# A four-layer graph network on one core: the edge network of the middle layers kept on 128 partitions

## The chip, the cores and the metric

The kernel runs on one core of one Trainium2 chip, in one launch. The metric is the device time of that launch in microseconds (us). Engines are called by the profile's names: PE is TensorE (PEld its weight loads), DVE VectorE, ACT ScalarE, POOL GpSimd, and SPq, ACTq and POOLq are the queues on which DMAs are issued.

## What is computed

Four graph layers update `x` (3125 nodes x 160 values: 64 scalars and 32 vectors of three) over 100,000 edges sorted by `dst`. Each adds its result to `x`. The two middle layers, L1 and L2, do per edge, with `k` = 8 and 16 features of the edge (L1 shown, L2 differs in scale factors and in a mean in place of a sum):

```python
h = silu(edge_scalars @ fcW1 * (1.0 / np.sqrt(RAD)))      # edges x 8 -> edges x 64
w = h @ fcW2 * (1.0 / np.sqrt(HID))                       # -> edges x 192
wA, wB, wC, wD = (w[:, :64], w[:, 64:128], w[:, 128:160], w[:, 160:192])
xs, xv = f_s[edge_src], f_v[edge_src]                     # the node's row, gathered
outA = wA * xs * y0
outD = wD * jnp.einsum('eud,ed->eu', xv, y1) * INV3
outB = wB[:, :, None] * xs[:, :, None] * y1[:, None, :]
outC = wC[:, :, None] * xv * y0[:, :, None]
agg = segment_sum(concatenate([outA, outD, outB, outC]), edge_dst)   # 384 values an edge
```

`h` and `w` are the inner values and the outputs of the "edge network". All is fp32.

## The kernel before

Edges are cut into 784 tiles of 128, with 48 more tiles that repeat edges at window borders. Four tiles make a group: 208 groups in L1 and L2, 196 in L3. The order of all work is written by hand: each engine has its own program, and `unrolled(count, [(lag, stage), ...])` lays out for step i every stage for group i - lag. Semaphores tie the engines together.

For a group g of L1 or L2 the engines do this:

- SP loads the edge features to `W.attr` (k x 512), two buffers.
- POOL gathers the node rows, `gathers_by_src` with the `indirect_dma_start` of L624: four gathers a group, each 128 rows of 640 bytes, to one of `DEPTH` = 4 buffers `W.got` in `fore`. Before a group's first gather it waits until the messages of four groups earlier are done. In L3 it does eight gathers a group, from `src_table` and `dst_table`, by the same line.
- PE has three stages, in this order in a step: `sums_by_window` for group i (L1233, four products 128 x 384 over 128 partitions, which add messages by destination; L1 has 384 columns, L2 385), `weights_by_hidden` for group i+2 (L1214, four products 128 x 192 over 64 partitions, giving `w`), `hidden_by_scalars` for group i+3 (L1200, one product 64 x 512 over 8 or 16 partitions, giving `h` before silu). In the trace each fp32 product shows as two weight loads and two matmuls ("passes" below).
- ACT does `hidden_out` (L848, silu from PSUM bank 0 to `W.hid`) and `rows_by_y0` (L864, four scalings of gathered rows).
- DVE (`edges_by_window`; its products go through a helper, L1446) makes the messages from `w` and the rows, and adds window sums to the accumulator. Every 32 windows (16 groups) it loads the next window numbers to registers.

PSUM: bank 0 holds the hidden product, banks 1 and 2 or 3 and 4 the weights (`wmm(b)`, two tiles to a bank), banks 5 to 7 the window sums.

L0 runs before them with a like loop, whose sums are scattered by POOL (L662); L3 after them, with two tensor products and an attention. At the start of the kernel ACT issues all weight loads (`wload`, L723) before the first square root of the layer norm (`root`, L715), for which DVE waits. `BY_Y0` splits `fc2_1` and `fc2_2` into four column pieces each.

## Time and profile before

| | |
|---|---|
| median of 3 timed runs | 7715.1 us (7669.87 to 7729.05) |
| profiled execution, span | 7980.6 us |
| mean granted TensorE clock | 0.904 |
| busy: PE, DVE, POOL, ACT | 88%, 82%, 67%, 46% |

The only time of the profiled execution is its span, from its first to its last instruction. It is 265.5 us (3.4%) above the median of the timed runs, which ran without the profiler. By stage of the program the profile has: set-up to about 130 us, L0 to about 1930, L1's edges from 2067 to 3185, L2's from 3313 to 4430, L3's from 4600 to 7350, L3's second pass and the end to 7980.6.

### The profile page before, as it was taken

How to read it: one execution, taken by the hardware profiler on the slowest of the kernel's cores; microseconds unless marked ns; L12 is line 12 of the kernel's file. 1: busy time of each engine (PE TensorE's matmuls, PEld its weight loads, DVE VectorE, ACT ScalarE, POOL GpSimd, SP SyncE). 2: the span in 40 equal slices, each digit the busy share in tenths (PEclk: the TensorE clock that was granted, in tenths of full speed). 3: DMA queues.
4: the chain of work that ended last, by engine and by line, in shares of the span. 5: the costliest groups of instructions: out<-in, count | busy, mean ns of one | idle time of the engine just before them, and what ended most of it. 6: DMA issues, size and time to landing. Idle time of an engine off the chain costs nothing. (4 is left out here: it accounts for less than half of the span.)

```text
span 7980.6 us, 110610 instructions
## 1 busy us (share of the span) xinstructions
PE 7037.4 (88%) x32406; PEld 4813.5 (60%) x32406; DVE 6580.0 (82%) x18417; ACT 3693.0 (46%) x9602; POOL 5364.8 (67%) x4078
## 2 busy tenths in 40 slices
PE   6999999997999999899999788888888888888488
PEld 3444444444555555555555477777787777777366
DVE  7999999996788888688888677777787777777785
ACT  2444444443333333433333355555555555555385
POOL 1777777773577777377777188888888888887000
PEclk7999999996899999799999778888888888888698
DMA  7999999998222222122222133322222222222263
GB/s 211 167 168 170 167 169 165 166 162 189 52 65 66 66 65 61 37 68 69 69 69 69 32 68 76 73 68 71 73 76 69 74 70 72 72 72 71 68 192 107
DMA packets 459687, 776.87 MB, mean 97 GB/s; under 512 B 96721, under 2 KB 310966, under 8 KB 458838
## 3 DMA queue, kind: packets, MB, share of 16 engines
q0 software_dynamic: 274944, 469.50, 32.1%
q1 hardware_dynamic: 180038, 299.69, 12.3%
q8 instruction: 269, 4.41, 0.2%
q14 instruction: 324, 2.65, 0.1%
q10 hardware_dynamic: 4112, 0.62, 0.1%
HBM read 464.60 MB, written 304.85 MB: 96 GB/s over the span
## 5 line engine op out<-in xcount | busy, mean ns | idle before, releaser
L1446 DVE TENSOR_TENSOR work<-work 128x256 f32<-128x256 f32 (+5 forms) x5726 | 2483.9, 472 | 70.3 <-DMA work<-src_sum 27.6
L624 POOL DMA_INDIRECT fore<-node_table,src_i x1664 | 1709.7, 1027 | 655.9 <-issue 504.4
L662 POOL DMA_INDIRECT src_sum<-work,put_i x832 | 1325.2, 1593 | 557.1 <-ACT work L836 384.6
L624 POOL DMA_INDIRECT fore<-src_table,src_i x784 | 1218.3, 1554 | 406.8 <-issue 238.6
L624 POOL DMA_INDIRECT fore<-dst_table,dst_i x784 | 1090.0, 1390 | 238.9 <-issue 238.9
L1233 PE MATMUL bank<-work 128*128 128x384 f32 (+1 forms) x3328 | 1198.8, 503 | 10.4 <-DVE work L1446 10.4
L1330 PE MATMUL bank<-ident,work 128*128 128x128 f32 x4704 | 733.5, 297 | 444.4 <-DVE work L1446 444.4
L1233 PEld LDWEIGHTS bank<-work 128*128 128x128 f32 x3328 | 603.2, 191 | 688.2 <-issue 313.6
L1446 DVE TENSOR_TENSOR work<-work,bank 128x384 f32 (+6 forms) x2080 | 908.0, 437 | 78.4 <-issue 70.7
L1330 PEld LDWEIGHTS bank<-ident,work 128*128 128x128 f32 x4704 | 572.3, 151 | 566.7 <-DVE work L1446 506.0
L848 ACT ACTIVATE work<-bank 64x512 f32<-64x512 f32 x416 | 245.8, 591 | 1436.6 <-PE bank L1200 1436.6
L1185 PE MATMUL bank<-work 128*128 128x480 f32 x1664 | 780.4, 604 | 3.0 <-DVE work L1446 2.8
L1446 DVE TENSOR_TENSOR work<-fore 128x640 f32<-128x640 f32 (+1 forms) x198 | 166.9, 843 | 621.7 <-DMA fore<-dst_table,dst_i 599.9
L1214 PEld LDWEIGHTS bank<-w_fc,work 64*128 64x128 f32 x3328 | 532.7, 188 | 237.8 <-issue 225.7
L1214 PE MATMUL bank<-w_fc,work 64*128 64x192 f32 x3328 | 656.1, 338 | 5.4 <-ACT work L848 5.4
L836 ACT ACTIVATE work<-bank 128x480 f32<-128x480 f32 x832 | 474.4, 570 | 303.0 <-PE bank L1185 236.6
L1446 DVE TENSOR_TENSOR work<-bank,aux 128x128 f32<-128x128 f32 (+1 forms) x1248 | 606.8, 487 | 0.0
L1446 DVE TENSOR_TENSOR work<-bank,work 128x256 f32<-128x256 f32 x832 | 405.7, 488 | 218.6 <-ACT work L864 218.6
L1185 PEld LDWEIGHTS bank<-work 128*128 128x128 f32 x1664 | 272.2, 192 | 519.3 <-issue 266.3
L864 ACT ACTIVATE work<-fore,y 128x160 f32<-128x160 f32 x1664 | 570.6, 415 | 0.0
L979 ACT ACTIVATE work<-bank 128x768 f32<-128x768 f32 x392 | 324.5, 828 | 488.0 <-PE bank L1330 487.9
L1200 PE MATMUL bank<-work,w_fc 8*64 8x512 f32 (+1 forms) x832 | 449.2, 619 | 14.8 <-DMA work<-in_edge_attr 14.8
(246 smaller groups left out, 13200.5 us busy)
## 6 DMA issues: line engine op xcount, KB each, us to landing
edge_h<-work SPq DMA_DIRECT2D x196, 320.0 KB, 2.3
work<-edge_h SPq DMA_DIRECT2D x196, 320.0 KB, 3.4
work<-keys SPq DMA_DIRECT2D x196, 256.0 KB, 5.8
fore<-node_table,src_i POOLq DMA_INDIRECT x1664, 2.7
work<-in_edge_attr SPq DMA_DIRECT2D x196, 128.0 KB, 5.9
src_sum<-work SPq DMA_DIRECT2D x4, 6240.0 KB, 37.5
work<-src_sum SPq DMA_DIRECT2D x100, 240.0 KB, 4.3
src_sum<-work,put_i POOLq DMA_INDIRECT x832, 5.9
```

Source lines behind the costliest of these rows:

```text
L624: return pool.indirect_dma_start(dst, None, table, bass.IndirectOffsetOnAxis(ap=idx, axis=0), bounds_check=bound, oob_is_err=True)
L662: pool.indirect_dma_start(src_sum[t], bass.IndirectOffsetOnAxis(ap=put_i[:, e:e + 1], axis=0), E.run[:, g % 2, t * 480:(t + 1) * 480], Non ...
L836: act.activation(E.run[:, b, t * f:(t + 1) * f], bank[:, 6 + n % 2, 0:f], ACT.Copy).then_inc(s.run_out, 1)
L848: act.activation(W.hid[0:64, b, :], bank[0:64, 0, :], ACT.Silu, scale=(8 ** -0.5, 0.25)[l - 1]).then_inc(s.hidden_out, 1)
L864: last = act.activation(W.by_y0[:, b, t, :], W.got[:, g % DEPTH, t, :], ACT.Copy, scale=y[:, e:e + 1, 0])
L979: act.activation(T.t1[:, h % 2], bank[:, 1:3, 0:384], ACT.Copy).then_inc(s.m1_in_sbuf, 1)
L1185: nc.tensor.matmul(bank[:, 6 + n % 2, 0:f], E.sel[:, b, t, :], E.msg[:, b, t * f:(t + 1) * f], start=True, stop=True).then_inc(s.run_mm, 1)
L1200: nc.tensor.matmul(bank[0:64, 0, :], wt[f"fc1_{l}"][:], W.attr[0:k, b, :], start=True, stop=True).then_inc(s.hidden_mm, 1)
L1214: last = nc.tensor.matmul(wmm(b)[:, t, 0:192], W.hid[0:64, b, t * P:(t + 1) * P], wt[f"fc2_{l}"][:], start=True, stop=True)
L1233: last = nc.tensor.matmul(o, W.sel[:, b, t, :], W.msg[:, b, t * f:(t + 1) * f], start=t == 2 * i, stop=t == 2 * i + 1)
L1330: last = nc.tensor.transpose(bank[:, to + t, i * P:(i + 1) * P], f[:, b, at + t, c0:c0 + P], ident[:])
L1446: return V_.tensor_tensor(o, p, q, op)
```

## The change

The inner values of the middle layers lay on 64 partitions by 512 edges. They now lie on 128 partitions by 256: edges 0 to 255 of a group on partitions 0 to 63, edges 256 to 511 on 64 to 127.

- `hidden_by_scalars`: two products of 64 x 256 in place of one of 64 x 512. The second writes PSUM partitions 64 to 127, so it uses the other half of the array's columns.
- `hidden_out`: one activation of 128 x 256 in place of 64 x 512.
- `weights_by_hidden`: the same four products, now in the order of tiles 0, 2, 1, 3. Tiles 0 and 1 read partitions 0 to 63, tiles 2 and 3 partitions 64 to 127, so by turns the upper and the lower half of the array's rows. Tiles 0 and 1 write one PSUM bank, 2 and 3 the other.
- `fc2_1` and `fc2_2` need their 64 rows on both halves: 128 partitions, and each piece loaded twice, eight more DMAs on ACT's queue at the start.

```diff
@@ weights
-        weight("fc2_1", 64, 192)
+        weight("fc2_1", P, 192)
-        weight("fc2_2", 64, 192)
+        weight("fc2_2", P, 192)
@@ window_views
-            v.hid = g(2, 512)
+            v.hid = g(2, 256)
@@ scalar engine, weight loads
-                for to, at, n in BY_Y0:
-                    n = min(n, wt[name].shape[1] - to)
-                    wload(wt[name][:, to:to + n], a[key][:, at:at + n])
+                k = a[key].shape[0]
+                for row in range(0, wt[name].shape[0], k):
+                    for to, at, n in BY_Y0:
+                        n = min(n, wt[name].shape[1] - to)
+                        wload(wt[name][row:row + k, to:to + n], a[key][:, at:at + n])
@@ hidden_out
-                    act.activation(W.hid[0:64, b, :], bank[0:64, 0, :], ACT.Silu,
+                    act.activation(W.hid[:, b, :], bank[:, 0, 0:256], ACT.Silu,
@@ hidden_by_scalars
-                    nc.tensor.matmul(bank[0:64, 0, :], wt[f"fc1_{l}"][:], W.attr[0:k, b, :], start=True, stop=True).then_inc(s.hidden_mm, 1)
+                    for half in range(2):
+                        last = nc.tensor.matmul(bank[64 * half:64 * half + 64, 0, 0:256], wt[f"fc1_{l}"][:],
+                                                W.attr[0:k, b, 256 * half:256 * half + 256], start=True, stop=True)
+                    last.then_inc(s.hidden_mm, 1)
@@ weights_by_hidden
-                    for t in range(GROUP):
-                        last = nc.tensor.matmul(wmm(b)[:, t, 0:192], W.hid[0:64, b, t * P:(t + 1) * P], wt[f"fc2_{l}"][:],
+                    for t in (0, 2, 1, 3):
+                        rows, at_hid = slice(64 * (t // 2), 64 * (t // 2) + 64), t % 2 * P
+                        last = nc.tensor.matmul(wmm(b)[:, t, 0:192], W.hid[rows, b, at_hid:at_hid + P], wt[f"fc2_{l}"][rows],
                                                 start=True, stop=True)
```

On PE, at the third and fourth group of L1, the program before has this order (L1200 hidden, L1214 weights, L1233 sums):

```order
L1200 MATMUL bank<-work,w_fc1_1 64x512
L1233 MATMUL bank<-work 128x384 x4
L1214 MATMUL bank<-w_fc2_1,work 128x192 x4
L1200 MATMUL bank<-work,w_fc1_1 64x512
L1233 MATMUL bank<-work 128x384 x4
```

The changed program at the same place (L1203 hidden, L1220 weights, L1239 sums):

```order
L1203 MATMUL bank<-work,w_fc1_1 64x256 x2
L1239 MATMUL bank<-work 128x384 x4
L1220 MATMUL bank<-w_fc2_1,work 128x192 x4
L1203 MATMUL bank<-work,w_fc1_1 64x256 x2
L1239 MATMUL bank<-work 128x384 x4
```

No stage moved past another; the hidden product became two of half the columns, and the four products of a weights stage differ in the partitions they read, which such rows do not show.

On ACT, among the weight loads at the start, this piece of the difference is the only one in which rows are added:

```order
 L723 DMA w_fc2_1<-in_L1_gnn_fcW2 64x64
 L723 DMA w_fc2_1<-in_L1_gnn_fcW2 64x32
+L723 DMA w_fc2_1<-in_L1_gnn_fcW2 64x64
+L723 DMA w_fc2_1<-in_L1_gnn_fcW2 64x32
+L723 DMA w_fc2_1<-in_L1_gnn_fcW2 64x64
+L723 DMA w_fc2_1<-in_L1_gnn_fcW2 64x32
+L723 DMA w_fc2_2<-in_L2_gnn_Wfc2 64x64
+L723 DMA w_fc2_2<-in_L2_gnn_Wfc2 64x32
+L723 DMA w_fc2_2<-in_L2_gnn_Wfc2 64x64
+L723 DMA w_fc2_2<-in_L2_gnn_Wfc2 64x32
```

Eight DMA issues more stand ahead of everything that ACT does later, the first square root (L715) among it.

## Rows read from the trace of the kernel before

**Rows 1.** Windows: L0, middles of L1 and L2, L3; us busy per engine.

```profile
core 0: us, PE busy (x) PEld busy (x) DVE busy (x) ACT busy (x) POOL busy (x), PEclk, DMA share, GB/s
130.00:1920.00 1790.00, 1672.20 (x5479) 838.97 (x5479) 1708.66 (x6888) 828.83 (x1473) 1325.16 (x832) 0.97 0.98 166
2100.00:3170.00 1070.00, 1065.86 (x3623) 584.17 (x3621) 945.21 (x2214) 374.91 (x1005) 825.27 (x804) 1.00 0.27 65
3345.00:4415.00 1070.00, 1066.00 (x3628) 583.54 (x3628) 944.84 (x2217) 374.93 (x1005) 824.99 (x805) 1.00 0.28 69
4600.00:7350.00 2750.00, 2312.65 (x15360) 2122.41 (x15361) 2122.83 (x5002) 1510.09 (x4228) 2278.87 (x1547) 0.86 0.28 72
```

**Rows 2.** Timeline of L1, PE and PEld: start us, us, engine, line, operation.

```profile
2803.70 2.85 PE L1233 MATMUL bank<-work 128*128 128x384 f32 x8
2806.48 1.56 PE L1214 MATMUL bank<-w_fc,work 64*128 64x192 f32 x8
2807.97 1.07 PE L1200 MATMUL bank<-work,w_fc 8*64 8x512 f32 x2
2808.97 0.59 PE L1233 MATMUL bank<-work 128*128 128x384 f32 x1
2806.48 0.29 PEld L1214 LDWEIGHTS bank<-w_fc,work 64*128 64x128 f32 x2 [0.55 <-issue]
2807.97 0.19 PEld L1200 LDWEIGHTS bank<-work,w_fc 8*64 8x64 f32 x2 [0.23 <-issue]
```

**Rows 3.** Timeline of L1, POOL, five gathers in a row.

```profile
2802.96 1.01 POOL L624 DMA_INDIRECT fore<-node_table,src_i  x1 [0.30 <-issue]
2804.28 1.01 POOL L624 DMA_INDIRECT fore<-node_table,src_i  x1 [0.30 <-issue]
2805.60 1.01 POOL L624 DMA_INDIRECT fore<-node_table,src_i  x1 [0.30 <-issue]
2806.91 1.01 POOL L624 DMA_INDIRECT fore<-node_table,src_i  x1 [0.30 <-issue]
2808.23 1.01 POOL L624 DMA_INDIRECT fore<-node_table,src_i  x1 [0.30 <-issue]
```

**Rows 4.** Waits in 2100 to 3170: who waited for whom, us, times, longest.

```profile
ACT work L848 <- PE bank L1200: 694.1, 201, 5.5
POOL fore L624 <- issue: 244.1, 801, 0.3
...
DVE work L1446 <- ACT work L864: 102.3, 181, 1.2
...
DVE work L1446 <- issue: 22.0, 15, 1.9
...
POOL fore L624 <- DVE work L1446: 0.9, 3, 0.3
```

**Rows 5.** Line L624 in 2100 to 3170: its DMAs' time to landing.

```profile
DMA to landing us min/median/max: 2.6/2.7/4.1
```

**Rows 6.** Waits in L3, 4600 to 7350.

```profile
DVE work L1446 <- DMA fore<-dst_table,dst_i: 591.1, 169, 13.2
...
POOL fore L624 <- issue: 471.4, 1547, 0.3
```

**Rows 7.** Timeline of the set-up: ACT's weight loads, the root, DVE behind it.

```profile
14.81 2.56 ACTq L723 DMA_DIRECT2D w_fc<-in_L_gnn_fcW  x4
...
17.39 2.56 ACTq L723 DMA_DIRECT2D w_fc<-in_L_gnn_Wfc  x4
...
19.99 2.01 ACTq L723 DMA_DIRECT2D w_rbf<-in_L_gnn_W_rbf  x4
...
25.04 0.24 DVE L1469 RECIPROCAL stats<-stats 128x13 f32<-128x13 f32 x1 [4.97 <-ACT stats L715]
...
36.92 0.21 ACT L715 ACTIVATE stats<-stats 128x12 f32<-128x12 f32 x1 [11.91 <-DMA w_lin_yz<-in_L_gnn_Wv_vlin]
...
37.16 0.23 DVE L1469 RECIPROCAL stats<-stats 128x12 f32<-128x12 f32 x1 [1.20 <-ACT stats L715]
```

**Rows 8.** Timeline: DVE's last work before the first barrier, SP's first behind it.

```profile
125.42 0.28 DVE L1707 TENSOR_SCALAR w_lin_yz<-w_lin_yz,w 128x128 f32<-128x128 f32 x1
127.56 1.31 SPq L515 DMA_DIRECT2D work<-keys  x3
```

**Rows 9.** Timeline of L1's end: last gather, last group's first message product, its sums.

```profile
3174.85 1.01 POOL L624 DMA_INDIRECT fore<-node_table,src_i  x1 [0.30 <-issue]
...
3180.16 0.55 DVE L1446 TENSOR_TENSOR work<-fore,y 128x384 f32<-128x384 f32 x1
...
3183.83 1.56 PE L1233 MATMUL bank<-work 128*128 128x384 f32 x4 [1.15 <-DVE work L1446]
```

**Rows 10.** Page, part 5: gathers of L1 and L2, of L3, weight loads.

```profile
L624 POOL DMA_INDIRECT fore<-node_table,src_i x1664 | 1709.7, 1027 | 655.9 <-issue 504.4
...
L624 POOL DMA_INDIRECT fore<-src_table,src_i x784 | 1218.3, 1554 | 406.8 <-issue 238.6
L624 POOL DMA_INDIRECT fore<-dst_table,dst_i x784 | 1090.0, 1390 | 238.9 <-issue 238.9
...
L1214 PEld LDWEIGHTS bank<-w_fc,work 64*128 64x128 f32 x3328 | 532.7, 188 | 237.8 <-issue 225.7
```

## The prediction

> **What bounds the kernel now.** I read the windows by stage first, then one group of L1 on each engine, then the waits. In L0 DVE is busy for 1708.66 of 1790 us [rows 1], and the change does not touch L0. In the middles of L1 and L2 PE is busy for 1066 of 1070 us at clock 1.00 [rows 1]: PE looks like the limit. The timeline gives a period of 2808.97 - 2803.70 = 5.27 us: 2.78 for the sums, 1.49 for the weights, 1.00 for the hidden product [rows 2].
>
> But POOL shows the same period. Four gathers start 2808.23 - 2802.96 = 5.27 us apart, each 1.01 us long with 0.30 before it [rows 3]. Over the whole stretch its 825.27 us busy, 244.1 us of such gaps and 0.9 us of waiting for DVE [rows 1, 4] sum to 1070.3 us, all of it. So POOL never waits for anybody in the profile: the gathers run free at 1070/804 = 1.331 us each, 5.32 a group (201 groups), and PE's 5.27 lies within 1% of that. Two engines are at their limit at once. DVE is third: it waits 102.3 us for ACT and 22.0 us otherwise [rows 4], so it needs (1070 - 124.3)/201 = 4.70 us a group, its register loads included, which stand in no row as busy.
>
> Now the profile against the timed runs. The profiled execution took 265.5 us more than the median. PE's and DVE's parts cannot give that much back: L0 has at most 1790 - 1708.66 = 81 us in which DVE is not busy, L1 and L2 together 8 us in which PE is not [rows 1]. At least 176 us must come from L3 and the parts between the layers. L3 in the profile is POOL's from end to end: 2278.87 us busy and 471.4 us of its 0.30 us gaps are 2750.3 of 2750 us [rows 1, 6], while DVE stands 591.1 us waiting for gathers [rows 6]. So I read it thus: without the profiler a gather is issued faster, and L1 and L2 are then held by PE alone, at 5.27 us. How much faster: 176 us over L3's 1568 gathers is 0.112 each, 1.317 down to 1.205, 4.82 us a group. All 265.5 us over all 4064 indirect DMAs of the kernel (1664 + 1568 [rows 10], 832 scatters [rows 1]) is 0.065 each, 5.01 a group. This is argued, not seen.
>
> **The change part by part.** The hidden product: two passes of 512 columns become four of 256, the same columns in all. If the halves of the array's columns work side by side, a half's two passes still follow each other, and only the second pass of one can lie under the first of the other: three quarters of 1.00 us, a saving of 0.25. If not, nothing. I take 0.15, nearer the full saving, since a pass has fixed parts too and its weight loads double (2 now take 0.19 us [rows 2]).
>
> The weights: eight passes in 1.49 us, 0.186 each. With row halves by turns the same pairing makes five steps of eight, 0.93 us, a saving of 0.56. The loads limit that: two loads take 0.29 us [rows 2] where one is 0.188 [rows 10], so they start 0.10 apart, eight need 0.8, and the last pass and the gap to the next stage come behind: about 1.1 us. I take a saving of 0.35; the ends are 0 and 0.56. PE then needs 5.27 - 0.50 = 4.77 us a group, between 4.46 and 5.27.
>
> The Trainium skill, page "TensorE: Matmul & The Clock Gate", section "The mechanism", speaks against the first half: a weight load overlaps running matmuls only where the row group differs, and both column halves read the same rows. By it the hidden product saves 0 and PE needs 4.92. The rows show both loads of the hidden product inside 0.19 us while its matmuls run 1.07 [rows 2], so here the second load did not wait for the first matmul.
>
> ACT's silu of 128 x 256 is shorter than that of 64 x 512, but ACT waits 694.1 us for that product in 1070 [rows 4]; the work that hides it is PE's, and it is worth nothing. It also could not cost: ACT has 695 us spare.
>
> The eight DMAs at the start: eight such issues take 5.2 us (14.81 to 19.99 [rows 7]), in front of the root for which DVE already waits 4.97 us. DVE falls back 5.2 us. Its second wait, 1.20 us, came from a weight that landed last, at about 36.9 [rows 7], from SP's queue; DVE now comes to that point 5.2 us later, so that most of the wait goes (I take 0.9): net 4.3 us. DVE is the last at the first barrier (125.70 us, SP goes on behind it [rows 8]), so the 4.3 us are on the path.
>
> The end of a layer: DVE takes up the last group at 3180.16, though its last gather, issued at 3174.85 and landing 2.7 us later [rows 5, 9], was there at 3177.6. PE's lag is the reason. With a faster PE 2.6 us go, in each of two layers: 5.2 us.
>
> **The sum.** For the profiled execution, where the gathers set 5.32 us before and after: 7980.6 + 4.3 - 5.2 = 7980 us, no change, with PE idle some 0.5 us a group. For the timed runs: three limits now lie close, PE 4.77, DVE 4.70 and the gathers between 4.82 and 5.01. Chains that share such a load do not run at the largest alone; before, 5.32 came out of 5.27. I take 4.96, near the middle of the gathers' bounds with that 0.05 on top. (5.32 - 4.96) x 416 groups = 150 us, less 4.3, and the lag's 5.2 is not counted again: 146 us. 7715 - 146 = 7569; I say 7570. With 4.82 it is 7511, with 5.06 it is 7611.
>
> **Rivals.**
> 1. *The gathers are as slow without the profiler.* Then L1 and L2 do not move: 7715 + 4.3 - 5.2 = 7714. For it: rows 3 as they stand, and that timed and profiled runs may differ by something between the layers. Against: L3's waits and the 176 us above. Chance 0.22.
> 2. *The products do not run side by side.* No row of before shows two products on different parts of the array, so nothing excludes it. PE stays at 5.27, and the start costs 4.3: 7719. Against stands the skill, page "TensorEngine Tiling (Array Packing)", section "Key Properties", by which different tiles load and multiply in parallel; no run here shows it yet. Chance 0.12.
> 3. *Slower: TensorE's clock.* A PE with pauses may lose its clock. L3 shows it: PE is busy 84% of the time and the granted clock is 0.86 [rows 1], that is 28% of the time at 1.2 and the rest at 2.4 GHz; in L1 and L2 PE is busy 99.6% and the clock is 1.00. With L3's clock, 4.77 us of PE work take 4.77/0.86 = 5.55 us a group: 0.23 x 416 = 96 us more, 7815. It decides from a clock of 0.90 down. Against: a PE that falls behind has no pauses any more, and in L0, busy 93%, the clock is 0.97 [rows 1]. Chance 0.09.
>
> **How the numbers follow.** My forecast (gathers faster without the profiler, products side by side) has 0.57, the rivals 0.22, 0.12 and 0.09. About 1% (77 us, 7638) is what a measurement of this kernel can tell from no change, its three runs lying 59 us apart. Of the forecast's 0.57 some 0.50 lie beyond 1%, the rest saves less; rivals 1 and 2 are within it but for a tenth of noise; rival 3 is slower. So faster 0.50, same 0.39, slower 0.11. The forecast's own range is 7500 to 7640. The range must reach rivals 1 and 2 with some of the spread of the timed runs: 7500 to 7735, which leaves out rival 3 and an underestimated gain.
>
> **What the profile of the changed kernel would show.** The span near 7980 us, though the timed runs fall: gathers in L1 still 1.32 us apart, POOL's busy time and gaps still filling the stretch, PE idle before L1239 with DVE as the releaser, and DVE waiting for the gathers' landing at the head of a group. The weights stage near 1.14 us and the hidden stage near 0.85; if the weights stage is still 1.49, rival 2 holds. DVE's first reciprocal near 30.2 us in place of 25.04. A clock in L1 clearly under 0.97 would speak for rival 3. The prediction is wrong if the timed runs move with the profile, both near their old times (rival 1), or if the profile's span itself falls by over 50 us, which would say that POOL's 1.317 us was set by PE or DVE after all.

## The result, and the profile after

| | before | after |
|---|---|---|
| median of 9 timed runs each, same chip | 7715.1 us (7669.87 to 7756.97) | 7765.83 us (7749.17 to 7828.48) |
| profiled execution, span | 7980.6 us | 7747.4 us |
| mean granted TensorE clock | 0.904 | 0.907 |

The ratio is 1.0086, 95% interval 1.0059 to 1.0113: the change makes the kernel slower by 0.9%, 51 us. The prediction was 7570 us, faster by 145. It was wrong in sign.

The windows after, for the stretches of [rows 1]:

```profile
core 0: us, PE busy (x) PEld busy (x) DVE busy (x) ACT busy (x) POOL busy (x), PEclk, DMA share, GB/s
130.00:1920.00 1790.00, 1674.02 (x5484) 840.23 (x5484) 1709.18 (x6889) 830.69 (x1476) 1323.38 (x832) 0.97 0.98 167
2100.00:3170.00 1070.00, 885.80 (x3899) 463.40 (x3898) 914.33 (x2145) 342.40 (x975) 832.32 (x780) 0.94 0.25 64
3345.00:4415.00 1070.00, 893.53 (x3896) 465.24 (x3896) 912.03 (x2138) 345.38 (x977) 831.99 (x782) 0.94 0.27 67
```

PE fell from 1065.86 to 885.80 us busy in L1's 1070, so the change did on TensorE what it says. But in the same 1070 us POOL made 780 gathers where it had made 804 [rows 1], and was busy longer for them (832.32 against 825.27). Fewer and longer gathers: that is the loss. The waits of the same stretch, to set beside [rows 4]:

```profile
ACT work L866 <- DMA fore<-node_table,src_i: 392.6, 177, 4.3
...
POOL fore L624 <- issue: 213.0, 699, 0.3
PE bank L1239 <- DVE work L1452: 182.3, 148, 4.0
DVE work L1452 <- DMA fore<-node_table,src_i: 135.2, 158, 2.7
...
POOL fore L624 <- DVE work L1452: 24.7, 81, 0.3
```

POOL's busy time and its two kinds of 0.30 us gaps are 832.3 + 213.0 + 24.7 = 1070.0 us: it still never stops. New are ACT and DVE waiting for the DMA: the gathers are now the only limit, and both engines start a group when its last gather lands. PE's part of one step, and what DVE and POOL do there (start us, us, engine, line, operation, idle before):

```profile
2805.13 0.92 PE L1220 MATMUL bank<-w_fc,work 64*128 64x192 f32 x8
2805.98 0.65 PE L1203 MATMUL bank<-work,w_fc 8*64 8x256 f32 x4
2806.56 2.85 PE L1239 MATMUL bank<-work 128*128 128x384 f32 x8
...
2809.34 0.92 PE L1220 MATMUL bank<-w_fc,work 64*128 64x192 f32 x8
...
2811.64 0.69 DVE L1452 TENSOR_TENSOR work<-in_window,column 128x512 f32<-128x512 f32 x1
2811.95 1.26 POOL L624 DMA_INDIRECT fore<-node_table,src_i  x1 [0.30 <-DVE work L1452]
...
2813.25 0.56 DVE L1452 TENSOR_TENSOR work<-fore,y 128x384 f32<-128x384 f32 x1 [0.46 <-DMA fore<-node_table,src_i]
2813.52 1.18 POOL L624 DMA_INDIRECT fore<-node_table,src_i  x1 [0.31 <-issue]
```

Weights take 2805.98 - 2805.13 = 0.85 us (1.49 before [rows 2]), the hidden product 2806.56 - 2805.98 = 0.58 (1.00), the sums 2.78 as before. PE needs 4.21 us a group. The last four rows show the two places of the loss. A gather that starts at 2811.95, while DVE compares window numbers (128 x 512, the **select**), takes 1.26 us instead of 1.01. The next starts at 2813.52, while DVE multiplies rows and y (128 x 384, called **t1** below), and takes 1.18. The groups of [rows 10] after:

```profile
L624 POOL DMA_INDIRECT fore<-node_table,src_i x1664 | 1773.8, 1066 | 656.3 <-issue 453.4
...
L1239 PE MATMUL bank<-work 128*128 128x384 f32 (+1 forms) x3328 | 1309.1, 540 | 383.4 <-DVE work L1452 380.8
```

A gather of L1 and L2 takes 1066 ns on average, 1027 before. With the 0.305 us between them that is 4 x 0.039 = 0.156 us a group, 65 us in 416 groups.

By stage, from the start times of the gathers in the traces (worked out from them; us from the first to the last gather of a layer, and the mean gather of L1 and L2). The last column, "over", adds up what the gathers of L1 and L2 that are longer than 1.06 us take above 1.012, in us; it is used further down:

```
                       L1       L2      L2 to L3     L3      gather ns    over
before, 1st chip     1107.7   1106.5     169.2     2784.8     1027        26.2
before_again         1108.0   1106.4     169.3     2411.0     1027        25.4
after                1140.1   1138.1     157.9     2499.6     1066        90.5
after_third          1141.3   1139.4     166.1     2407.8     1067        93.3
t0_first             1124.4   1130.9               2412.6     1052        65.7
select_moved_b       1118.0   1117.1     159.3     2408.3     1040        45.6
both_moved           1104.8   1105.7               2409.4     1025        21.6
before_moved         1110.8   1110.3               2412.9     1021        12.6
same_rows            1138.1   1137.0               2404.4     1064        87.4
pe_padded            1137.9   1140.3     159.8     2404.1     1066        89.6
pe_balanced          1139.3   1141.9     157.8     2441.7     1068        89.4
pe_above             1132.0   1134.4     161.4     2453.8     1059        74.4
pe_seven_b           1252.0   1143.8     169.1     2409.0     1056        74.1
pe_eight_b           1254.4   1144.0     166.5     2404.7     1062        83.0
```

L1 and L2 got 32.4 and 31.6 us longer, the way from L2 to L3 shorter by 11.3: 53 us, and the timed runs say 51. L3 is left out of this sum, because the profile of before has an unusually long one (next section). The first scatter of L0 starts at 156.4 us, at 156.6 before, so this pair shows no loss at the start. Over all profiles it starts at 155.9 us on average in the four of the kernel before and its variants (154.1 to 156.8), and at 158.4 in the sixteen of the changed kernel and its variants (156.0 to 159.3): the start costs some 2.5 us.

### The profile page after: what moved, and what is told of

Read it like the earlier page. It is cut to its first block and busy times, and to the rows that moved or that the text cites. A ratio compares the mean times of both kernels' runs of the same rounds, so it can differ in the third digit from the quotient of the medians.

```text
span 7747.4 us, 112282 instructions
## 1 busy us (share of the span) xinstructions
PE 6602.2 (85%) x33238; PEld 4479.1 (58%) x33238; DVE 6586.9 (85%) x18417; ACT 3648.7 (47%) x9602; POOL 5141.9 (66%) x4078
## 5 line engine op out<-in xcount | busy, mean ns | idle before, releaser
L624 POOL DMA_INDIRECT fore<-node_table,src_i x1664 | 1773.8, 1066 | 656.3 <-issue 453.4
L1239 PE MATMUL bank<-work 128*128 128x384 f32 (+1 forms) x3328 | 1309.1, 540 | 383.4 <-DVE work L1452 380.8
L624 POOL DMA_INDIRECT fore<-src_table,src_i x784 | 1042.2, 1329 | 395.5 <-issue 238.6
L1239 PEld LDWEIGHTS bank<-work 128*128 128x128 f32 x3328 | 648.0, 205 | 952.2 <-DVE work L1452 540.3
L624 POOL DMA_INDIRECT fore<-dst_table,dst_i x784 | 981.1, 1251 | 238.9 <-issue 238.9
L1187 PEld LDWEIGHTS bank<-work 128*128 128x128 f32 x1664 | 273.0, 192 | 519.9 <-issue 266.2
L850 ACT ACTIVATE work<-bank 128x256 f32<-128x256 f32 x416 | 159.7, 384 | 709.4 <-PE bank L1203 709.2
L1452 DVE TENSOR_TENSOR work<-fore,y 128x384 f32<-128x384 f32 x416 | 235.2, 565 | 303.3 <-DMA fore<-node_table,src_i 302.3
L1147 PE MATMUL bank<-w_fc,work 64*128 64x224 f32 x1664 | 427.1, 377 | 1.4 <-ACT work L817 1.4
L827 ACT ACTIVATE work<-bank 128x448 f32<-128x448 f32 x416 | 226.4, 544 | 425.2 <-PE bank L1147 425.0
L1328 PE MATMUL bank<-w_rbf,work 16*128 16x224 f32 x1568 | 405.3, 378 | 12.7 <-DMA work<-in_edge_attr 10.7
```

Source lines behind the costliest of these rows:

```text
L624: return pool.indirect_dma_start(dst, None, table, bass.IndirectOffsetOnAxis(ap=idx, axis=0), bounds_check=bound, oob_is_err=True)
L827: act.activation(E.w[:, b, 2 * i:2 * i + 2, :].rearrange("p t c -> p (t c)"), bank[:, 1, 0:448], ACT.Copy).then_inc(s.fc_out, 1)
L1147: last = nc.tensor.matmul(bank[:, 1, t * 224:(t + 1) * 224], E.hid[0:64, b, at:at + P], wt["fc2_0"][:], start=True, stop=True)
L1187: nc.tensor.matmul(bank[:, 6 + n % 2, 0:f], E.sel[:, b, t, :], E.msg[:, b, t * f:(t + 1) * f], start=True, stop=True).then_inc(s.run_mm, 1)
L1239: last = nc.tensor.matmul(o, W.sel[:, b, t, :], W.msg[:, b, t * f:(t + 1) * f], start=t == 2 * i, stop=t == 2 * i + 1)
L1328: last = nc.tensor.matmul(bank[:, 0, t * 256:t * 256 + 224], T.rb[0:16, b, (at + t) * P:(at + t + 1) * P], wt["rbf"][:], start=True, stop= ...
```

## The experiments

They ran on five occasions; times are compared only with the kernel before on the same chip and occasion.

### Does the profile exceed the timed runs?

The kernel before once more, unchanged.

> The kernel before, unchanged, for a second profile of it. Theory A (the first profile of before was a rare, long execution of L3, whose 2785 us from first to last gather stand against 2500 us in the profile of the changed kernel): this profile's span lies near 7715 us, L3 near 2520 us, while L1 and L2 again take 1107 us from first to last gather, with gathers 1.317 us apart. Theory B (the profiler slows the gathers): the span is again near 7980 us.

Measured: 7606.77 us (10 runs), ratio to the other runs of before 1.001 [0.9997, 1.0023], span of the profiled execution 7607.4. The profiler costs nothing that can be seen, and gathers of L1 take 1027 ns with and without that long L3. The first profile is longer than this one by 373.2 us, all of it in L3: 2784.8 us there and 2411.0 here, and 2499.6 in the profile of the changed kernel, on the first chip too. In part 5 of this profile and of the first one ([rows 10]) the gathers of L3 differ, 1292 and 1175 ns here, 1554 and 1390 there:

```profile
L624 POOL DMA_INDIRECT fore<-node_table,src_i x1664 | 1709.5, 1027 | 657.3 <-issue 503.8
L624 POOL DMA_INDIRECT fore<-src_table,src_i x784 | 1013.3, 1292 | 407.1 <-issue 238.8
L624 POOL DMA_INDIRECT fore<-dst_table,dst_i x784 | 921.1, 1175 | 239.0 <-issue 239.0
```

The longer gathers are 0.477 us for a pair, 374 us in 784 pairs: all of the difference. So it was one execution with a long L3. The traces also show what its gathers waited for: DVE, in the way that is worked out under "Which operation of DVE holds the gathers?". Why DVE's work lay so badly in that one execution stays open.

### What would each engine take without the fourth gather?

Both kernels with three gathers a group in L1 and L2 (a quarter of the gathered rows is left out there, and DVE and ACT use what the buffer holds). Their waits for a group's gathers count three in place of four; the cut shows the loop alone.

```diff
-                    for t in range(GROUP):
+                    for t in range(GROUP - 1):
```

> The kernel before, where L1 and L2 gather only three of a group's four tiles (the fourth keeps old rows, so the result is not the reference's). POOL needs 3.95 us a group. If PE is a limit of its own at 5.27 us a group, as its timeline says, L1 and L2 still take 207 x 5.27 = 1091 to 1105 us from first to last gather; if they were POOL's alone they fall towards DVE's 4.7 us, 975 to 1000 us.

> The changed kernel with three of four gathers in L1 and L2 (the same work left out). POOL needs 3.95 us, PE 4.2 us (2.78 + 0.85 + 0.57), DVE about 4.7 us a group: L1 and L2 take 975 to 1010 us each from first to last gather. This is what the faster PE would be worth if the gathers did not set the pace: 90 to 120 us a layer. If they stay near 1090, something else than POOL holds the changed kernel.

Measured, one run each: before 7605.6 us against 7602.28, nothing gained; after 7334.53. The windows of L1, first before, then after:

```profile
2100.00:3000.00 900.00, 896.23 (x3044) 491.49 (x3042) 798.64 (x1860) 315.20 (x845) 547.64 (x508) 0.99 0.20 50
```

```profile
2100.00:3000.00 900.00, 824.61 (x3828) 435.07 (x3826) 888.10 (x2107) 316.92 (x959) 630.63 (x577) 0.99 0.23 57
```

Before, PE alone still holds L1 at 1099.4 us, 5.31 a group. After, the layer takes 968.0 us and DVE is at its limit (888.10 of 900). So the change is worth 131 us a layer to PE, and none of it can be had while four gathers take 5.27 us a group.

### Does the order of the row halves matter?

Products in the order of tiles 0, 1, 2, 3 again, all else as changed.

```diff
-                    for t in (0, 2, 1, 3):
+                    for t in range(GROUP):
```

> The changed kernel with the second product in the order of tiles 0, 1, 2, 3: two products in a row on the same half of the array's rows, then two on the other. If side-by-side work of different halves makes the gain on PE, the weights stage goes from 0.85 us back towards 1.49 (one of three neighbours differ: about 1.3), PE needs about 4.7 us a group, still under the gathers' 5.27, and the time stays near 7765 under theory H. If the faster PE as such lengthens gathers in proportion (rival P), the time falls about half way to 7715.

Measured: 7653.4 us, ratio 1.0072 [1.0047, 1.0097], L1 1138.1. PE's weights stage in its timeline:

```profile
2804.99 0.93 PE L1220 MATMUL bank<-w_fc,work 64*128 64x192 f32 x8
2805.85 0.65 PE L1203 MATMUL bank<-work,w_fc 8*64 8x256 f32 x4
```

0.86 us, as with alternation, where about 1.3 was expected. The saving of the weights stage comes without the alternation, then: two products on one half followed by two on the other do as well. In the trace's single records the eight matmuls of a stage start in four pairs, 13 ns apart within a pair here and 6 with alternation, where before they started one by one, 0.163 us apart. That fits two halves that each work through their own products, whatever the order of issue. Which part of the change does give it (the two halves at all, or the banks) was not taken apart.

### Is a fast PE itself the cause?

The hidden pair computed three times (useless work, same values).

```diff
-                    for half in range(2):
+                    for half in (0, 1) * 3:
```

> The changed kernel with the pair of hidden products issued three times over (same result, written again), so that PE needs about 4.2 + 2 x 0.48 = 5.2 us a group as before. Theory H: DVE is no longer let loose by the landing of gathers but by PE, the SBUF product leaves the gathers' edges, L1 and L2 take 1107 to 1115 us each, the time falls to about 7715. If only the work as such on other rows and columns of the array matters (rival P), gathers stay at 1.066 us and the time near 7765.

Measured: 7651.38 us, 1.006 [1.0036, 1.0083], gathers 1066 ns. PE then needs 5.07 us a group, still less than the gathers' 5.27, and the loss is unchanged. These are the numbers of rival P, but this run can't tell it from the other theory, since the gathers still set DVE going. The next runs can: they change nothing on PE.

### Which operation of DVE holds the gathers?

In the changed kernel a group's t1 starts when the group's fourth gather has landed: 2.66 us after that gather's start, the middle half of all groups between 2.63 and 2.74 us. In the kernel before, the middle half lies between 4.25 and 5.80: there PE sets DVE's pace. DVE's work does not drift along the gathers there; it keeps its place for tens of groups (in L2 4.47 to 4.51 us behind for 64 groups, later 5.70 to 5.86 for 80, as means of 16). The mean gather by its position in the group, worked out from the traces (L1, ns):

```
                     1st    2nd    3rd    4th
before              1030   1023   1027   1033
after               1117   1117   1024   1011
t0_first            1131   1032   1015   1015
select_moved_b      1048   1044   1021   1049
both_moved          1025   1012   1043   1019
```

First: t1 behind t0, DVE's product of rows and `w` that writes PSUM, in the changed kernel.

```diff
-                    tt(t1, xv, bc(yy[:, :, 1:4], 3, V), ALU.mult).then_inc(dve_own, c.step())
-                    parts = c.n
...
+                    tt(t1, xv, bc(yy[:, :, 1:4], 3, V), ALU.mult).then_inc(dve_own, c.step())
+                    parts = c.n - 1
+                    dve.wait_ge(dve_own, parts + 1)
+                    tt(t2, t1[:, :, 0, :], t1[:, :, 1, :], ALU.add).then_inc(dve_own, c.step())
                     dve.wait_ge(dve_own, parts)
-                    tt(t2, t1[:, :, 0, :], t1[:, :, 1, :], ALU.add).then_inc(dve_own, c.step())
-                    dve.wait_ge(dve_own, parts + 1)
```

> The changed kernel with DVE's two products behind the wait for a group's gathers swapped: first the one on the weights in PSUM (128 x 256), then the one of rows and edge attributes (128 x 384, both operands in SBUF), which so starts some 0.34 us later against the landing. Theory H (a gather on POOL is held while that SBUF product runs at the gather's begin or end; in the changed kernel the product starts where a gather begins): gathers go back to 1.03 us in the mean, L1 and L2 to 1107 us each from 1140, the time to about 7700. Rival P (the faster products on PE lengthen the gathers, whatever DVE does): gathers stay at 1.066 us in the mean, time near 7765.

Measured: 7634.7 us, 1.0032 [1.0015, 1.005]. L1 took 1124.4 us and L2 1130.9, not the 1107 expected. The second gather of L1 is back from 1117 to 1032 ns, the first still held, by the select. Moving t1 took back half of the loss in L1 and less in L2.

Then both moves, the select also behind the addition of finished window sums.

```diff
-                    select(g, W.sel[:, b]).then_inc(dve_own, c.step())
...
+                    select(g, W.sel[:, b]).then_inc(dve_own, c.step())
```

> The changed kernel with two DVE operations of L1 and L2 moved, none added: the product of rows and edge attributes one place later (as in the run with the swap), and the comparison of 128 x 512 that makes the selection matrix from the head of a group to behind the add of its window sum. Theory H' (a gather is held at its begin as long as DVE runs an operation whose operands all lie in SBUF; 76% of gathers that began in that comparison and 61% of those that began in that product were longer than 1.06 us, and none of those that began in a product with a PSUM operand): both now lie between two begins, gathers are 1.02 us in the mean, L1 and L2 take 1096 to 1100 us each against 1107 before and 1139 after the change, and the time is 15 to 30 us under the kernel before. Rival P (the faster products lengthen the gathers): no change against 1139.

> The kernel before with the same two DVE operations moved. PE still needs 5.27 us a group, so under theory H' DVE drifts against the gathers by the small difference of 5.27 and 5.268 and settles free of them, as before: L1 and L2 1105 to 1110 us each, time within 0.2% of before. If the moves themselves bring the gain of the other kernel, L1 and L2 fall to 1096 to 1100 us here too.

Measured: changed kernel with both moves 7588.2 us (11 runs), ratio to before 0.9982 [0.997, 0.9994]; kernel before with both moves 7606.04, 1.0005 [0.9991, 1.0018]. Windows of both_moved:

```profile
2100.00:3170.00 1070.00, 904.59 (x4026) 475.08 (x4024) 962.08 (x2215) 352.69 (x1009) 824.62 (x806) 0.96 0.27 66
```

806 gathers in 1070 us in place of 780. The two moves give 35 us in L1 of the changed kernel (1104.8; 1096 to 1100 was expected), with nothing changed on PE: the loss hangs on the order of DVE's operations. In the kernel before they give nothing (1110.8 against 1107.7). That does not show that its gathers are free of DVE's operations; PE leaves room for 8 us at most (1099.4 in before_3gathers). The gathers do get shorter, 1021 ns in place of 1027, and in 2100 to 3170 POOL now waits for buffers, where it had waited 0.9 us [rows 4]:

```profile
POOL fore L624 <- DVE work L1446: 14.7, 13, 2.1
```

both_moved is the only version measured with all its gathers that is faster than the kernel before, by 0.2%.

The select alone was moved on two occasions, since on the first of the two every kernel was slow, the one before at about 8065 us.

> The changed kernel with only the select moved behind the addition of the finished window sums; the product of rows and y stays first in the message chain. Theory: the gather at position 0 of a group is no longer held (mean about 1.03 us instead of 1.12), the one at position 1 still is (1.10 to 1.14), so the mean gather is about 1.045 and a layer about 1122 us from first to last gather; in all about 7600 + 2 x 14 - 10 = 7618 us. Rival (only the two moves together bring anything, because what counts is how long DVE needs for a group and not which operation meets a gather): 1138 a layer, 7650 us.

> The changed kernel itself once more, beside the kernel before and the other variants. Theory (DVE starts a group's messages when its fourth gather lands, and so its operations without a PSUM operand meet the begin of the next gathers): 1138 us from first to last gather of L1 and of L2, mean gather 1.065 us, as in the first profile of it; against 1108 for the kernel before that is 2 x 30, less the 11 us that the way from L2 to L3 gets shorter: 7600 + 50 = 7650 us. If the lengthening belonged to one execution only (rival), L1 and L2 come out otherwise by 10 us or more and the ratio to before is within 0.3% of 1.

Measured there: before 8065.18, after_again 8075.19, 1.0016 [0.9992, 1.004], select_moved 8084.16, 1.0018 [0.9985, 1.005]. L1 took 1268 and 1271 us. The waits of after_again in 2100 to 3170 have rows that no other profile has:

```profile
ACT work L850 <- remote: 391.3, 56, 12.0
...
DVE bank L1452 <- remote: 73.0, 45, 2.7
```

Engines stop for up to 12 us and the trace shows nothing on this core that ends it. The gathers pace nothing there, and those runs decide nothing. The cause was not found. Again on another occasion:

> Only the select moved, on a chip where the gathers set the pace. Theory: position 0 of a group is no longer held (mean 1.03 us in place of 1.12), position 1 still is (1.10 to 1.14); mean 1.045, about 1122 us a layer, in all 18 us above the kernel before. Rival (only both moves together bring anything): 1138 a layer, 50 us above the kernel before.

> The changed kernel on another chip than the last, as the base of the runs beside it: where engines don't stop (kernel before at 7600 to 7715 us), 1138 us from first to last gather of L1 and of L2, mean gather 1.065 us, 7640 to 7660 us in all (or 50 above the kernel before). On a chip like the last (kernel before at 8065), 1268 a layer.

Measured: select_moved_b 7611.2 us, 1.0004 [0.9994, 1.0013], L1 1118.0; after_third, one run, 7684.69 against 7609.14 for before, L1 1141.3, so the lengthening is there again. The select alone is worth 22 us a layer, somewhat more than expected (1122), but the second gather at 1044 ns contradicts the expectation that it would stay at 1100 to 1140. With the select out of the way t1 starts less regularly behind the fourth gather (middle half 2.67 to 3.03 us, 2.63 to 2.74 before), and meets fewer gathers.

Over eleven profiles with undisturbed L1 and L2 (the fourteen of the table by stage without before_again, pe_balanced and pe_above), by what DVE was doing 0.1 us after a gather's start (worked out from the traces; numbers of gathers, share longer than 1.06 us, mean ns):

```
select, 128x512, both inputs in SBUF       1896    95%    1243
t1, 128x384, both inputs in SBUF           1812    47%    1138
128x128, both inputs in SBUF (work, work)  1169    20%    1031
an input or the output in PSUM           >11000     0%    1012
nothing                                    2409     0%    1012
```

The first two rows, and a fifth of the third, are the held gathers. Two more readings of the same traces say how they are held. What decides is which of the two starts first. Of the gathers under t1, 806 began when it had run for at least 0.06 us and had 0.15 us or more to go: 97% of them are long. For 625 more t1 began only after the gather had begun: not one is long. Under operations with PSUM, 8371 gathers began in the same way, and none is long. And a held gather ends a fixed time after the operation. In L1, L2 and L3 of the sixteen profiles with undisturbed L1 and L2 (the fourteen, before_3gathers and after_3gathers), 17,559 gathers are longer than 1.06 us, and 99.5% of them end 0.885 us (within 0.010) after the end of a DVE operation with both inputs in SBUF; none does so after one that touches PSUM. So a gather is let in when such an operation ends, and then takes 0.885 us more. In the rows shown for the changed kernel the select ends at 2812.33 and the gather under it at 2813.21, t1 at 2813.81 and the gather under it at 2814.70.

With that the loss adds up. The column "over" grows from 26.2 to 90.5 us, by 64.3, and L1 and L2 together by 64.0. In every row but three, L1 and L2 together are 2 x 831 x 1.317 = 2189 us and that column, within about 3 us. The three are before_moved, pe_seven_b and pe_eight_b, in which POOL waits for buffers. The long L3 of the first profile adds up too: its gathers longer than 1.06 us take 722 us above 1.012, those of before_again 347, and the difference of 374 is all that L3 was longer. Some wait there for two or more such operations in a row, up to 3.7 us.

The Trainium skill, page "SBUF — State Buffer", section "Who interferes with whom", says that a DVE instruction with two SBUF inputs contends with a GpSimd instruction that reads SBUF, and that one with at most one SBUF input, outside the 2-port perf modes, does not. The trace agrees: long gathers in the first three rows, none in the other two. The same section infers that a `tensor_tensor` does not hold up descriptor generation; the indirect gathers here were held, by 0.23 us on average under the select. The measurement decides.

### Would a PE at the gathers' period give the time back?

Useless work on PE up to and past the gathers' 5.27 us. First seven hidden products, and eight (`(0, 1) * 4`):

```diff
-                    for half in range(2):
+                    for half in (0, 1, 0, 1, 0, 1, 1):
```

> The changed kernel with TensorE made slower by useless work: seven hidden products a group in place of two (the first two written three times over, the second once more). By the three products of each half measured before, a half product costs about 0.22 us, so TensorE needs 2.78 + 0.85 + 0.57 + 5 x 0.22 = 5.30 us a group, about what the four gathers take undisturbed (5.27). Theory: TensorE sets the pace again, DVE gets its work from it and not from the landing, and the gathers get back to a mean of 1.025 to 1.035 us; L1 and L2 take 208 x 5.30 = 1102 to 1112 us each from first to last gather, so the kernel with more work is FASTER than the changed one by 50 us or more: about 7600. Rival (the gathers were made longer by something else in the change, the layout of the inner values or the shorter weight stage): the layers stay at 1138 and above, 7650 us or more.

> As the run with seven hidden products, now eight (each half four times): TensorE needs 2.78 + 0.85 + 0.57 + 6 x 0.22 = 5.51 us a group, clearly more than four undisturbed gathers. Theory: L1 and L2 go by TensorE, 208 x 5.51 = 1146 us each, and POOL waits some 0.2 us a group; its gathers keep a fixed phase to TensorE's work, and their mean says whether DVE's operations meet them at this phase too: 1.02 to 1.04 if not. About 7600 + 2 x 38 - 10 = 7666 us. Rival (gathers set the pace whatever TensorE does): 1138 a layer.

> Seven hidden products a group in place of two, as before on the other chip: TensorE needs about 5.30 us a group, what four undisturbed gathers take (5.27). Theory (phase of DVE against the gathers): mean gather back to 1.025 to 1.035 us, 1102 to 1112 us from first to last gather of L1 and of L2, so with more work FASTER than the changed kernel by 50 us: within 0.2% of the kernel before. Rival (something else in the change makes the gathers longer): mean 1.065 and 1138 or more a layer, 50 us or more above the kernel before.

> Eight hidden products a group: TensorE about 5.51 us a group, more than four undisturbed gathers. Theory: TensorE's pace, 208 x 5.51 = 1146 us a layer, and gathers of 1.02 to 1.04 us unless the fixed phase to TensorE's work meets them as well. Rival (gathers set the pace whatever TensorE does): 1138 a layer, mean 1.065.

Measured on the disturbed occasion 8215.76 and 8223.92 us, which decide nothing; on the other 7803.49, 1.0263 [1.0244, 1.0283], and 7813.59 (one run). All numbers missed. First, seven products took as long as eight, in either kernel's timeline:

```profile
2806.96 1.94 PE L1203 MATMUL bank<-work,w_fc 8*64 8x256 f32 x14
```

```profile
2808.13 1.94 PE L1203 MATMUL bank<-work,w_fc 8*64 8x256 f32 x16
```

A product on one column half costs as much as a pair on both, 0.435 us, not half of it. So PE needed 5.50 us in both, and L2 took 208 x 5.50 = 1144, as measured. Second, L1 took 1252 us, with PE busy for all of 1070. Windows of pe_seven_b, and a sums stage of its L1:

```profile
2100.00:3170.00 1070.00, 1070.00 (x5287) 587.82 (x5285) 839.84 (x1941) 291.80 (x883) 744.71 (x709) 0.91 0.24 58
...
2788.95 4.54 PE L1239 MATMUL bank<-work 128*128 128x384 f32 x8
```

The stage takes 4.54 us where it takes 2.85 at 2.4 GHz: the granted clock in it is 0.62, so part of it ran at 1.2, right behind 1.94 us of hidden products over 8 partitions. In L2, whose hidden products go over 16 partitions, the same kernel kept 5.51 us a group from group 16 on, at a granted clock of 0.99 (3480 to 4550). That the partitions make the difference is not shown. Third, in L2 the gathers were long although PE set the pace: the fourth of each group 1172 ns in pe_seven_b, the third 1211 in pe_eight_b, the others near 1012 to 1051. There the long gathers are a result of PE's pace and cost nothing: in L2 of pe_eight_b the mean of 1072 ns makes 4 x (1.072 + 0.305) = 5.51 us a group, PE's own period, and POOL never waits. POOL runs ahead until one gather of each group falls under a DVE operation that lengthens it to PE's period, and stays there. The kernel before looks the same: with gathers of 1022 to 1026 ns in the stretches in which DVE keeps its place, a group takes 5.31 to 5.32 us, and PE alone takes 5.31. That the holds keep the two together is a reading of the traces; no run was made for it.

The last two kernels double the weights products and add a narrower hidden pair, of 128 and of 192 columns.

```diff
-                    for half in range(2):
+                    for half, width in ((0, 128), (1, 128), (0, 256), (1, 256)):
...
-                    for t in (0, 2, 1, 3):
+                    for t in (0, 2, 1, 3) * 2:
```

> The changed kernel with useless work on TensorE: the four weights products done twice and, before the hidden pair, an extra pair of half its width. By the stages measured, 2.78 + 2 x 0.85 + 0.57 + 0.22 = 5.27 us a group, the period of the kernel before. Theory (the loss comes from DVE being set going by the landing at a fixed phase): DVE is paced by TensorE again, its phase to the gathers drifts, mean gather 1.025 to 1.04 us, 1103 to 1120 us from first to last gather of L1 and of L2: with more work faster than the changed kernel by 20 to 35 us a layer, and within 0.3% of the kernel before. Rival (the gathers follow DVE's order of operations whatever paces it): mean 1.06 and about 1138 a layer, 0.6% above the kernel before.

> The same with the extra pair three quarters wide: 5.05 + 0.33 = 5.38 us a group, 0.11 more than four undisturbed gathers. Theory: TensorE sets 208 x 5.38 = 1119 us a layer plus the 5 to 10 us of its stops; POOL waits now and then for a buffer. The changed kernel takes 1138, so this one too is faster with more work if nothing else holds the gathers. Rival: 1138 or more.

Measured: 7701.62 us, 1.006 [1.0038, 1.0082], L1 1139.3; and 7704.09, 1.0047 [1.0032, 1.0062], L1 1132.0. PE's stages of pe_balanced:

```profile
2804.33 2.85 PE L1239 MATMUL bank<-work 128*128 128x384 f32 x8
...
2807.11 1.57 PE L1220 MATMUL bank<-w_fc,work 64*128 64x192 f32 x16
...
2808.61 0.87 PE L1203 MATMUL bank<-work,w_fc 8*64 8x128 f32 x8
```

2.78 + 1.50 + 0.80 = 5.08 us, not the 5.27 aimed at: the doubled stage costs 0.65 more, not 0.85. So the point at which PE's period equals the gathers' was not hit. The numbers are those of the rival in the expectation (mean 1.06, about 1138 a layer, 0.6%), but t1 still starts 2.67 us behind the fourth gather in L1 (median), set going by the landing, so the theory's condition was not met and stays untested. What the two runs show is that at 5.08 us the loss is whole, and at 5.18 (2.77 + 1.50 + 0.91, pe_above) about a fifth of it is gone.

## Why the prediction was wrong, point by point

**The step that failed first** is "Now the profile against the timed runs": "without the profiler a gather is issued faster". It took one execution's excess of 265.5 us, put it in L3, where the second profile finds it too, and made it a property of the profiler and of every gather. DVE's 591.1 us of waiting for gathers in L3 [rows 6], which it took as support, were real: the gathers there had themselves been held by DVE, for 722 us where before_again has 347. before_again shows 7607.4 us with the profiler and 7606.77 without, and 7747.4 is the span of after with 7765.83 in its timed runs. The gathers of L1 and L2 take 1.012 + 0.305 us at their shortest in every run, so four of them never take less than 5.27 us, with the profiler or without. The term for it, 4.96 us a group, was 5.49. Rival 1, which had a chance of 0.22, had this right: 7714 us.

**What no step priced** is why it came out 52 us above rival 1 and not at it. The sum for the profiled execution took the gathers' period as fixed, 5.32 before and after, and the reading behind it was that "the gathers run free at 1070/804 = 1.331 us each". Free they take 1.317; the rest were holds, which no row of waits shows, because a held gather counts as busy. The prediction said that a freed PE leaves "DVE waiting for the gathers' landing at the head of a group", which came true (135.2 us in L1), but it did not ask what DVE then does at the moment at which the next gathers begin. It is mostly the select and t1, and they lengthen two gathers of four by 0.1 us each on average. That these two operations hold the gathers is shown by the two moves and by the ends of the held gathers; together the holds make 64.3 of the 64.0 us. That DVE's start at the landing is what brings them under the gathers is read from the place of t1 (2.63 to 2.74 us behind the fourth gather against 4.25 to 5.80). A run with PE exactly at the gathers' period would have tested it and is missing.

**Products side by side**: right in direction, small in size. The weights stage saves 0.64 us where the estimate was 0.35 and its upper end 0.56; the hidden product 0.42 where it was 0.15 and 0.25. PE needs 4.21 us, below the lower bound of 4.46. The bound "five steps of eight" assumed that only a product's neighbour can share its time, by turns; same_rows shows the turns to be irrelevant. Rival 2 falls. The rule of the Trainium skill that was weighed against the hidden product (page "TensorE: Matmul & The Clock Gate", section "The mechanism", no overlap of a weight load within one row group) would have left the product at 1.00 us; the trace shows 0.58.

**Start-up**: the reciprocal at 30.18 us and a second wait of 0.34 came out as forecast (30.2, and 1.20 less 0.9):

```profile
30.18 0.24 DVE L1475 RECIPROCAL stats<-stats 128x13 f32<-128x13 f32 x1 [9.93 <-ACT stats L715]
...
41.44 0.23 DVE L1475 RECIPROCAL stats<-stats 128x12 f32<-128x12 f32 x1 [0.34 <-ACT stats L715]
...
128.08 0.29 DVE L1713 TENSOR_SCALAR w_lin_yz<-w_lin_yz,w 128x128 f32<-128x128 f32 x1
130.23 1.31 SPq L515 DMA_DIRECT2D work<-keys  x3
```

The first barrier came 2.67 us later (128.37 against 125.70 [rows 8]), not 4.3 (a register load on DVE in front of it took 1.85 us where it had taken 4.69), and the first scatter of L0 on this pair no later at all. Over all profiles it came 2.5 us later. The term should have been followed to the first work that waits behind the barrier, not to the barrier.

**End of a layer**: the last gather of L1 starts at 3206.01 and t1 at 3208.64, 2.63 us later, 5.31 before [rows 9]; the forecast of 2.6 us less was right. From L1's last gather to L2's first it was 1.3 us less, and from L2's to L3's 11.3 on this chip but 3.1 in after_third; what makes the second vary was not looked into.

**Clock, rival 3**: the granted clock in L1 did fall, from 1.00 to 0.94, as forecast for a clock under 0.97. It cost next to nothing there: PE has 1.28 us to spare in a group of 5.49, and the holds alone make up the loss. pe_seven_b shows what it costs where PE is the limit: 6.03 us a group in L1, 5.51 in L2.

## What to carry to other kernels

When two engines are at their limit together, freeing one gives nothing, and it also takes away what paced a third: ask what that engine will be doing each time the other one begins. Look at long gathers for the DVE operation that runs at their start, and put operations with both inputs in SBUF where the gathers don't begin. Here L3 is the larger case: in 4600 to 7000 of before_again POOL never stops (1925.0 us busy and 475.3 of its gaps), and the holds of L3 are 347 us. DVE is busy for 2150.8 of these 2400 us, so an estimate of what moves there could give is at most 249 us; nobody tried it. An excess of one profiled execution over the timed runs is one draw until a second profile repeats it.

## What the runs showed of the hardware

An indirect gather of 128 rows on POOL, 1.012 us by itself, is held by a fp32 `tensor_tensor` on DVE with both inputs in SBUF that began before it (mean 1.243 us under 128 x 512, 1.138 under 128 x 384), and ends 0.885 us after that operation; one that begins after the gather does not hold it (0 of 625), and one that touches PSUM does not either (0 of 8371). Products of 64 columns' width on the two column halves of the array run side by side: one half alone takes 0.435 us for 256 columns, and so do both (seven products 1.94 us, eight 1.94). The order of tiles on row halves makes no difference to that (0.85 and 0.86 us for four products). The clock of TensorE can fall while PE has no pause in its records: 0.91 in L1 of pe_seven_b, busy 1070.00 of 1070.00 us, with sums stages of 4.54 us.
